# Slot tables of the lone attention block: one filler matmul a unit, layer norm of tile 0 in slots 12 to 16, five weight chunks split ahead of the first feed-forward block

## What is computed

```python
h = _L0_tok_ref(x, emb_table, norm_weight, proj_weight)
h = h + _L0_attn_ref(_layernorm(h, axis=-1), wq, wk, wv, wo)     # 32 heads of 16, 8 key heads, causal
h = h + _L0_ffn_ref(_layernorm(h, axis=-1), w_gate, w_up, w_down)  # silu(gate) * up, hidden 2048
```

## Time and profile before

| | us |
|---|---|
| median of 3 runs | 728.16 |
| the profiled execution's own time | 729.07 |
| its span, first to last instruction | 727.3 |
| TensorE matmul busy (x6309) | 697.0 (96%) |
| VectorE busy (x1038) | 415.8 (57%) |
| ScalarE busy (x722) | 350.7 (48%) |
| GpSimd busy (x402) | 298.8 (41%) |

### The profile page before, as it was taken

The page is one execution under the profiler, slowest core; times in us unless marked ns, Lnnn a source line. Parts: engine busy times, 40 slices in busy tenths (PEclk is TensorE's granted clock), DMA queues, the critical chain, the costliest instruction groups (busy, mean ns, idle before and its releaser), DMA issues.

```text
span 727.3 us, 16210 instructions
## 1 busy us (share of the span) xinstructions
PE 697.0 (96%) x6309; PEld 528.2 (73%) x6309; DVE 415.8 (57%) x1038; ACT 350.7 (48%) x722; POOL 298.8 (41%) x402
## 2 busy tenths in 40 slices
PE   8629989999999999999999999999999999999998
PEld 4427769985798659964898479865996489847873
DVE  6885689885665456563655456545656465543320
ACT  6865458872366216641565136621664056512320
POOL 7030112332366516753375436651675337521220
PEclk9958999999999999999999999999999999999999
DMA  8958310001200120003000110012000300000000
GB/s 330 405 173 302 142 47 1 2 2 46 75 2 1 46 75 2 3 1 105 15 2 2 60 60 3 1 46 75 2 2 1 106 15 2 3 15 15 1 1 30
DMA packets 10459, 40.37 MB, mean 56 GB/s; under 512 B 1808, under 2 KB 2576, under 8 KB 8592
## 3 DMA queue, kind: packets, MB, share of 16 engines
q1 hardware_dynamic: 6912, 25.44, 9.1%
q0 software_dynamic: 3328, 13.11, 5.8%
q10 hardware_dynamic: 144, 0.79, 0.3%
HBM read 29.89 MB, written 9.44 MB: 54 GB/s over the span
## 4 chain that ended last, share of the span: by engine, by line
PE 86%; DVE 7%; ACT 2%; DMA 2%; issue 1%; SPq 0%; POOL 0%; DVEq 0%; POOLq 0%
PE banks L1071 15%; PE banks L1073 15%; PE banks L1072 15%; PE banks L1155 6%; PE banks L1157 6%; PE banks L1156 6%; PE banks L1025 4%; PE banks L1043 3%; PE banks L1014 2%; PE banks L1104 2%; PE banks L1106 2%; PE banks L1105 2%; PE banks L1049 1%; PE banks L1120 1%; PE banks L1050 1%
## 5 line engine op out<-in xcount | busy, mean ns | idle before, releaser
L1073 PE MATMUL banks<-xnT_and_h,ffn_weights 128*128 128x256 f16 x1024 | 279.1, 273 | 0.0
L1071 PE MATMUL banks<-xnT_and_h,ffn_weights 128*128 128x256 f16 x1024 | 278.9, 272 | 0.1
L1072 PE MATMUL banks<-xnT_and_h,ffn_weights 128*128 128x256 f16 x1024 | 279.0, 272 | 0.0
L366 POOL TENSOR_TENSOR gated_split<-gate_work,gated_split 128x256 f16<-128x256 f32 x128 | 86.4, 675 | 261.1 <-ACT gated_split L514 261.1
L370 POOL TENSOR_TENSOR weights_split<-weights,weights_split 128x512 f16<-128x512 f32 x96 | 110.9, 1156 | 0.0
L1071 PEld LDWEIGHTS banks<-xnT_and_h,ffn_weights 128*128 128x128 f16 x1024 | 101.0, 99 | 11.9 <-DVE xnT_and_h L864 0.6
L502 ACT ACTIVATE gate_work<-banks,scales 128x256 f32<-128x256 f32 x128 | 60.5, 472 | 100.1 <-PE banks L1073 99.9
L1073 PEld LDWEIGHTS banks<-xnT_and_h,ffn_weights 128*128 128x128 f16 x1024 | 100.0, 98 | 11.7
L1072 PEld LDWEIGHTS banks<-xnT_and_h,ffn_weights 128*128 128x128 f16 x1024 | 99.9, 98 | 11.3
L814 DVE SCALAR_TENSOR_TENSOR weights<-weights,counts_T 128x512 f32<-128x512 f32 x128 | 87.4, 683 | 14.3 <-ACT weights L510 14.1
L510 ACT ACTIVATE weights<-banks,scales 128x512 f32<-128x512 f32 x128 | 87.2, 681 | 14.5 <-PE banks L1025 14.5
(11 more groups left out here) (238 smaller groups left out, 1091.5 us busy)
## 6 DMA issues: line engine op xcount, KB each, us to landing
ffn_weights<-in_ffn_w SPq DMA_DIRECT2D x12, 1024.0 KB, 15.7
out_rows_dram<-ffn_weights SPq DMA_DIRECT2D x16, 256.0 KB, 2.0
xnT_and_h<-in_wqkv SPq DMA_DIRECT2D x1, 1536.0 KB, 8.9
local_table<-gated_split SPq DMA_DIRECT2D x2, 640.0 KB, 6.5
local_table<-xnT_and_h SPq DMA_DIRECT2D x2, 640.0 KB, 3.6
gated_split<-in_projT SPq DMA_DIRECT2D x4, 256.0 KB, 3.7
ffn_weights<-in_wo SPq DMA_DIRECT2D x1, 1024.0 KB, 10.8
token_table<-weights_split ACTq DMA_DIRECT2D x1, 768.0 KB, 8.8
```

Of the source, the lines that this page charges most:

```text
L366: g.tensor_tensor(gtl[:, j, :], g2[j % 2], gth[:, j, :], ALU.subtract).then_inc(gt_lo, 1)
L1071: t.matmul(o, wh, xTh[m % 2][:, c, :], start=c == 0, stop=False)
L1072: t.matmul(o, wh, xTl[m % 2][:, c, :], start=False, stop=False)
L1073: last = t.matmul(o, wl, xTh[m % 2][:, c, :], start=False, stop=c == DC - 1)
```

## The change

It edits only the tables by which the loops place steps in slots.

```diff
-FIRST_SLOTS = dict(yt=(11, 18), wo=(13, 19), ln=(16, 20), rs=(17, 20), xhat=(19, 20), xn=(20, 21), xl=(21, 21), fetch=(17, 20), m=(22, 3))
+FIRST_SLOTS = dict(yt=(10, 18), wo=(11, 19), ln=(12, 20), rs=(13, 20), xhat=(14, 20), xn=(15, 21), xl=(16, 21), fetch=(13, 20), m=(22, 3))
-HI_FIRST = {16: 0, 17: 1, 20: 2, 21: 3}
-LOW_FIRST = {19: (0,), 21: (1,), 22: (2,), 23: (3,)}
-HI_NEXT = {i - 4: i for i in range(4, NCH)}
-FILL = {0: 5, 1: 3, **{s: 2 for s in range(2, 16)}, 20: 8, 21: 5}
+HI_FIRST = {16: 0, 17: 1, 18: 2, 19: 3, 20: 4}
+LOW_FIRST = {16: (0,), 17: (1,), 18: (2,), 19: (3,), 23: (4,)}
+HI_NEXT = {i - 5: i for i in range(5, NCH)}
+FILL = {0: 5, 1: 3, **{s: 1 for s in range(2, 16)}, 20: 8, 21: 5}
```

## The result

The changed kernel takes 736.69 us (median of 8 executions, 732.58 to 755.42) where the kernel before, run beside it, takes 728.50: a ratio of the means of 1.0093, 95% interval 1.0073 to 1.0114. It is slower by some 7 to 8 us, not by 2.1. The forecast had the sign and missed the size: 736.69 lies above its range, which ended at 732.8. The first profiled execution, the one of 755.42 us, had a clock of 0.95 from 59 us to its end wherever it was not at 0.50, which no other had; the ratio leaves it out, and the rows here are of the second profile (737.61 us, span 735.9).

A forecast was written before the change was run, and what follows sets the result against it. TensorE was taken to bound slots 2 to 15, a handshake chain the stretch behind; the change made VectorE's queue delay tile 1's ln by 2.08 us, the rest 0. Sum +2.1 on 728.16: 730.2 us, range 728.2 to 732.8.

The forecast's parts named there:

- Parts 1 to 5: Fewer fillers, earlier yt and wo, earlier layer norm of tile 0, earlier chunks, unchanged chain behind: together +2.1 us.
- the last division: VectorE, behind chunk 0's low half: starts at 89.07 instead of 87.09 us, 1.98 later.
- tile 1's ln: VectorE, behind two chunks in the wait for wo: starts at 95.07 instead of 92.99 us, 2.08 later.
- the gate: Phase 1's first gate matmul on TensorE: near 101.4 us instead of 99.30, after an unchanged chain of 6.31.
- fillers at 0.215: TensorE, slots 2 to 15: each filler removed saves 0.215 us, 14 of them 3.0 us.
- the wait for y: TensorE, slot 10: yt of tile 0 waits 1.08 us for y, whose last division is at line 828.
- unit 13's values: TensorE, slot 15: these values wait 0.3 us for unit 13's weights from VectorE.
- xn: TensorE, slot 15: tile 0's xn waits 2.35 us at the queue's head for xhat from VectorE.
- the chain from weights step 12 to xn: VectorE, units 12 to 15: weights steps, ln, division, rs and xhat take 6.46 us; xn starts at 85.19.
- rival (a): Clock falls to 1.2 GHz for about 4 us at TensorE's new wait: +1.3 to +2 more, 731.5 to 732.3 us; 18%.
- (b): Smaller loss: y of tile 0 is in time, so 1.28 us do not appear; +0.8, 729.0 us; 22%.
- (c): Faster: VectorE has room, TensorE stays the bound through slot 17, the fillers' 3.0 us return; -2.8, 725.4 us; 12%.

The follow-up runs named there:

- a9: Changed kernel with 11 fillers in slot 14, filling only TensorE's wait for xn of tile 0; 734.89 us against 728.72 for the kernel before, ratio 1.0078.
- a4: Changed kernel with 6 fillers in slot 9 and 11 in slot 14, filling TensorE's waits; 730.71 us against 729.06 for the kernel before, ratio 1.0025.
- a2: Kernel before with one filler instead of two in slots 2 to 15, nothing else changed; 727.11 us against 729.06, ratio 0.9967.
- a1: Changed kernel run again without any edit; 737.46 us against 729.06 for the kernel before, ratio 1.0109.
- a7: Kernel before with no filler in slots 2 to 15; 733.75 us against 728.65, ratio 1.0054.
- a3: Changed kernel with two fillers again in slots 2 to 15; 735.72 us against 729.06 for the kernel before, ratio 1.0082.
- a6: Kernel before with one filler in slots 2 to 11 and two in 12 to 15; 727.09 us against 728.65, ratio 0.9976.
- a12: Kernel before with one filler in slots 2 to 11, two in 12 to 15, 6 added across slots 18, 20, 21; 726.64 us against 728.72, ratio 0.9970.

## Why the prediction was wrong

**Parts 1 to 5, the sum of +2.1, were right.** a9's profile shows the forecast's schedule to the first gate matmul at full clock:

```profile
57.70 1.02 PE L1043 MATMUL banks<-v_full_one,weights 128*128 128x17 f32 x8
...
87.74 0.20 DVE L821 RECIPROCAL rden<-banks 128x8 f32<-128x8 f32 x1
...
93.90 0.75 DVE L850 SCALAR_TENSOR_TENSOR xnT_and_h<-banks,scales,token_rows 128x512 f32<-128x512 f32 x1
...
100.21 0.28 PE L1071 MATMUL banks<-xnT_and_h,ffn_weights 128*128 128x256 f16 x1
```

In the kernel before the values of unit 0 started at:

```profile
59.04 1.02 PE L1043 MATMUL banks<-v_full_one,weights 128*128 128x17 f32 x8
```

Counted from there, the last division comes at 30.04 for 28.05 (2.0 later, 1.98 forecast), tile 1's ln at 36.20 for 33.95 (2.25, for 2.08), and the gate at 42.51 for 40.26 (2.25, for 2.1). The times agree: four executions of this schedule have a mean clock of 0.988, two of a4 (729.57, 730.80) and two of a9 (730.41, 730.52), mean 730.3; eleven of the kernel before average 728.2 there, 2.1 us less. In the rows of the changed kernel and its variants: fillers at 0.215 (14 of them 3.0 us in a2), the wait for y (0.93 for 1.08), for unit 13's values (0.17 for 0.3), for xn (2.15 for 2.35), the chain from weights step 12 to xn (6.49 for 6.50), the division behind chunk 0 (a4). Tile 1's ln follows the last low half, at 93.76, without a gap in a4.

**The step that failed is rival (a), in its chance and its price.** It gave the clock's fall 18% and "for about 4 us". The forecast's sum had the clock at 2.4 GHz throughout and put its fall at nothing. Ten of the twelve executions of the changed kernel had more time at 1.2 GHz than the prologue explains, and the profiled one 7 + 13.7 us of it behind 60 us. The price came from the start of phase 0, where the clock returned after 4.0 us of unbroken work; but that work was mostly fillers of 512 columns. After the fall at 85.7 TensorE's work is values of 17 columns, one filler, tile 1's transposes and gram matmuls of 128, and 11.4 us of such work did not bring the clock back. It came back at 79 and at 99.4 us, both times within the twelve 512-column matmuls of wo, which had begun at 75.50 and 98.03. On the path, comparing a1 with a4 and counting from the start of the values of unit 0 (58.70 and 58.23 us), the first fall costs (82.12 - 58.70) - (78.51 - 58.23) = 3.1 us up to tile 0's ln, and the second (101.51 - 82.12) - (94.42 - 78.51) = 3.5 more up to tile 1's: 6.6 us beside the schedule's 2.2, which makes 8.9 counted from there. The units began 0.3 us sooner than before (58.70, for 59.04), so the gate is 8.5 later.

**The argument for and against the rival was wrong.** For it spoke the 2.35 us wait, but the second fall begins ahead of that wait. Against it, the prediction said that a slot with one filler idles no longer than before. True, and beside the point: a2 and a7 show the clock falling with TensorE busy throughout. I had treated the fillers as a pure cost, as if only idle time mattered for the clock; two of them held it through the plain units in every profile here, with none it was lost in 3.4 us. What exactly starts a fall, and why the same program has executions with and without one, stays open.

The Trainium skill, page "TensorE: Matmul & The Clock Gate", table "Why this matters for your kernels", warns of idle gaps between bursts of matmuls. a3 lost the clock in a wait of 1.89 us, shorter than the gaps that the table warns of, and a2 in none, so that advice is not enough here. The section "A second HAM failure mode: psum-queue depth-cycling", which the prediction cited for the rival, is nearer, with a clock that swings although no gap is long. But it, too, puts this down to short idle times, and a2 and a7 have none in the profile.

**The other rivals.** (b), no wait for y, and (c), the fillers' 3 us come back with the norm moved, did not occur: the wait for y and the wait for xn are in every profile of these slots that doesn't fill them. The fillers' gain is real only with the old slots (a2, a6, a12).

## What to carry to other kernels

Filler matmuls have two prices: what they take from TensorE's queue, and what the clock takes when they are gone; a cut of fillers is judged by the clock's row in several executions, not by the unit's sum. Before a late step is pulled forward into an engine that works in order, add up what it does to the steps behind it: 3.6 us of VectorE steps in two slots of 1.4 us became a 2.15 us wait of TensorE, and the stretch of thin units and waits cost more through the clock (6.6 us) than by its schedule (2.2). Where a wait can't be avoided, work of no use placed in it costs nothing: tile 1's ln is at 36.19 us in a4, with the wait for y filled, and at 36.20 in a9, with it open. Filling both waits gave back 6.8 us here.

## What the runs showed of the hardware that was not expected

The clock falls while TensorE has no idle time in the profile, if the work is small matmuls: at 83.8 us in a2 and after 3.4 us of filler-less units in a7, where it then stayed low for 24 us of unbroken work. Nor does it fall alike in each execution of one program: a9 had two of six at the clock of a profile without a fall, and the four others some 5 us slower; and a wait of 1.92 us was followed by a fall in a4's profile and by none in a9's. A kernel near this edge has no single time, and its executions sorted by mean clock tell more than the median alone. The prologue, untouched here, differs by 10 us at 1.2 GHz between executions, worth 1.7 us.
